# Rows of v in two column halves: stores, gathers, splits and the last products of a graph transformer layer

## The reference, cut to what matters

```
x = x + gnn(layernorm(x)) + mix(layernorm(x))
def fff(x, node_w, node_b, w1, b1, w2, b2):        # tree of depth 4, 16 leaves of width 64
    leaf = route(x, node_w, node_b)
    hidden = relu(x @ w1[leaf] + b1[leaf])
    return hidden @ w2[leaf] + b2[leaf]
q, k, v = fff(h, q_...), fff(h, k_...), fff(h, v_...)      # h = layernorm(x)
attn = softmax(q @ k.T / 32)                               # 384 x 384
x = x + attn @ v                                           # 384 x 1024
```

## Time and profile before

| | us |
|---|---|
| median of 3 runs | 727.94 (725.6 to 729.39) |
| the profiled execution, its own time | 726.86 |
| its span (first to last instruction) | 725.1 |
| PE busy | 702.6 (97%) |
| DVE busy | 476.5 (66%) |
| ACT busy | 402.0 (55%) |
| POOL busy | 229.2 (32%) |
| mean granted TensorE clock | 0.997 of full speed |

### The profile page before, as it was taken

The page is one execution under the profiler, slowest core; times in us unless marked ns, Lnnn a source line. Parts: engine busy times, 40 slices in busy tenths (PEclk is TensorE's granted clock), DMA queues, the critical chain, the costliest instruction groups (busy, mean ns, idle before and its releaser), DMA issues.

```text
span 725.1 us, 11736 instructions
## 1 busy us (share of the span) xinstructions
PE 702.6 (97%) x4490; PEld 669.4 (92%) x4490; DVE 476.5 (66%) x957; ACT 402.0 (55%) x692; POOL 229.2 (32%) x203
## 2 busy tenths in 40 slices
PE   3999999999999999999999999999999998999987
PEld 3989999998999999999999999998899998889886
DVE  6758774874777477766666565656766466787543
ACT  5455556464565565768686775422523457677340
POOL 4634332232332332227022274470004511422120
PEclk9999999999999999999999999999999999999998
DMA  5421635413313223231313152234135749896242
GB/s 212 160 107 59 231 138 211 176 60 120 109 67 117 73 102 117 90 118 58 117 59 117 59 209 73 109 121 138 41 136 193 272 164 378 307 413 220 117 145 88
DMA packets 21766, 105.15 MB, mean 145 GB/s; under 512 B 5696, under 2 KB 6080, under 8 KB 12912
## 3 DMA queue, kind: packets, MB, share of 16 engines
q1 hardware_dynamic: 12880, 80.84, 30.4%
q0 software_dynamic: 8544, 23.41, 8.9%
q10 hardware_dynamic: 288, 0.14, 0.1%
HBM read 92.71 MB, written 18.06 MB: 153 GB/s over the span
## 4 chain that ended last, share of the span: by engine, by line
PE 87%; DVE 6%; ACT 3%; DMA 2%; issue 1%; DVEq 0%; ACTq 0%
PE g_bank L1772 37%; PE g_bank L1797 12%; PE o_bank L1847 4%; PE t_bank L1836 4%; PE s_bank L2150 2%; PE s_bank L1824 2%; PE s_bank L1825 2%; PE g_bank L1726 2%; PE s_bank L2398 2%; PE s_bank L2360 2%; PE s_bank L2358 2%; PE s_bank L2359 2%; PE t_bank L2150 2%; DVE w_lo L1138 1%; PE g_bank L2332 1%; PE t_bank L2251 1%
## 5 line engine op out<-in xcount | busy, mean ns | idle before, releaser
L1772 PE MATMUL g_bank<-act_hi,w_hi 128*128 128x384 f32 x488 | 170.0, 348 | 0.0
L1772 PE MATMUL g_bank<-act_hi,w_lo 128*128 128x384 f32 x488 | 163.7, 335 | 0.0
L1772 PE MATMUL g_bank<-act_lo,w_hi 128*128 128x384 f32 x488 | 163.4, 335 | 0.0
L1138 DVE TENSOR_TENSOR w_lo<-raw,w_hi 128x2048 fp32r<-128x2048 f32 x58 | 137.3, 2367 | 36.0 <-ACT w_hi L675 34.0
L675 ACT ACTIVATE w_hi<-raw 128x2048 fp32r<-128x2048 f32 x67 | 128.1, 1912 | 30.3 <-PE s_bank L2150 12.5
L490 POOL DMA_INDIRECT edge_table<-ew,eidx x51 | 68.2, 1336 | 164.3 <-DMA edge_table<-ew,eidx 158.0
L1772 PEld LDWEIGHTS g_bank<-act_hi,w_hi 128*128 128x128 f32 x488 | 91.8, 188 | 2.7 <-issue 2.6
L1772 PEld LDWEIGHTS g_bank<-act_lo,w_hi 128*128 128x128 f32 x488 | 91.9, 188 | 0.0
L1772 PEld LDWEIGHTS g_bank<-act_hi,w_lo 128*128 128x128 f32 x488 | 91.6, 188 | 0.0
L437 POOL TENSOR_TENSOR w_lo<-raw,w_hi 128x2048 fp32r<-128x2048 f32 x10 | 47.0, 4695 | 103.5 <-ACT w_hi L675 97.2
L1275 DVE TENSOR_TENSOR pT_lo<-t_bank,pT_hi 128x384 fp32r<-128x384 f32 x96 | 50.6, 554 | 33.6 <-ACT pT_hi L768 33.2
(11 more groups left out here) (324 smaller groups left out, 1643.5 us busy)
## 6 DMA issues: line engine op xcount, KB each, us to landing
raw<-wstream_dram SPq DMA_DIRECT2D x68, 1024.0 KB, 4.8
xg<-xs POOLq DMA_DIRECT2D x12, 512.0 KB, 7.9
ys<-y_ring POOLq DMA_DIRECT2D x12, 512.0 KB, 4.6
x_sb<-x_dram SPq DMA_DIRECT2D x3, 512.0 KB, 5.0
y_acc<-x_dram POOLq DMA_DIRECT2D x3, 512.0 KB, 5.7
out_dram<-out_sb SPq DMA_DIRECT2D x6, 256.0 KB, 2.0
edge_table<-ew,eidx POOLq DMA_INDIRECT x51, 2.5
edge_table<-mask POOLq DMA_DIRECT2D x1, 576.0 KB, 3.5
```

Source lines behind the costliest of these rows:

```text
L1138: V.tensor_tensor(flat(w_lo[to][:, :, :]), raws[raw_slot(n.base)], flat(w_hi[to][:, :, :]), ALU.subtract) \
L1772: last = mm(out, w2[a], x2[b], start=k == 0 and a + b == 0, stop=not after and k == KT - 1 and a == 1)
```

## The change

The ring of v rows is the same, but every step behind it works on half a tile's columns:

- Stores: for each of pairs 6 to 11 POOL stores the first half as soon as ACT has taken it (waits for y_act only), then the second half (waits for y_dve), into two DRAM arrays yv[0] and yv[1] of 512 columns. `take_y` of pairs 9 to 11 waits for the store of its own half only.
- Gathers: the first halves of the three tiles (when all first halves are stored and k's transposes are done), then the second halves. Six indirect DMAs of 128 x 512 in place of three of 128 x 1024.
- Splits: ACT and DVE split the three first halves between the softmax of tiles 0 and 1, and the second halves later.
- Products: LAST gives their order: (tile 0, first half), (tile 1, first half), (0, second), (1, second), (2, first), (2, second). The first needs only the first halves of v (vf_ready of 3), the third needs all six. `last_T(2)` moves one product later, and DVE's `take_last(2)` moves behind the first sum.

```diff
+V_PAIRS = 1 * PAIRS
+LAST = ((0, 0), (1, 0), (0, 1), (1, 1), (2, 0), (2, 1))
...
+            def store_v(i, half):
+
+                p = i - V_PAIRS
+                pool.wait_ge((y_act, y_dve)[half], i + 1)
+                pool.dma_start(yv[half][p * P:(p + 1) * P, :], y_at[i][:, half * 512:(half + 1) * 512]) \
+                    .then_inc(v_out[half][p % NT], 16)
+
+            def bring_v(half):
+
+                if half == 0:
+                    pool.wait_ge(kT_full, K_FILLS)
+                for s in v_out[half]:
+                    pool.wait_ge(s, 16 * (PAIRS // NT))
+                for t in range(NT):
+                    nc.gpsimd.indirect_dma_start(y_ring[:, t, half * 512:(half + 1) * 512], None, yv[half],
+                                                 rows_of(2, t), bounds_check=ROWS - 1,
+                                                 oob_is_err=False).then_inc(v_in[half][t], 16)
...
-            for i in range(PAIRS, 2 * PAIRS):
-                store_pair(i)
-            bring_back(1)
+            for i in range(V_PAIRS, V_PAIRS + PAIRS):
+                for half in range(2):
+                    store_v(i, half)
+            for half in range(2):
+                bring_v(half)
...
-            def take_v(t):
-                act.wait_ge(back_in[t], 32)
-                nc.scalar.activation(vf_hi[:, t, :], y_ring[:, t, :], ACT.Copy).then_inc(vf_hi_ready, 1)
+            def take_v(half, t):
+                cols = slice(half * 512, (half + 1) * 512)
+                act.wait_ge(v_in[half][t], 16)
+                nc.scalar.activation(vf_hi[:, t, cols], y_ring[:, t, cols], ACT.Copy).then_inc(vf_hi_ready, 1)
...
             last_exp(0)
+            act.wait_ge(y_full, 2 * (V_PAIRS + PAIRS))
+            for t in range(NT):
+                take_v(0, t)
             last_exp(1)
-            take_v(0)
+            take_v(1, 0)
+            take_v(1, 1)
             take_last(0)
-            take_v(1)
-            take_v(2)
+            take_v(1, 2)
             last_exp(2)
...
             normalise(pf_ring, Index(S_FFN0), 0)
+            for t in range(NT):
+                take_v(0, t)
             last_max(1)
             normalise(pf_ring, Index(S_FFN0 + 1), 1)
-            take_v(0)
+            take_v(1, 0)
+            take_v(1, 1)
             take_last(0)
-            take_v(1)
             last_max(2)
-            take_v(2)
+            take_v(1, 2)
             normalise(pf_ring, Index(S_FFN0 + 2), 2)
             take_last(1)
-            take_last(2)
...
+                if i == 1:
+                    take_last(2)
...
-            for i in range(2 * NT):
-                t, half = divmod(i, 2)
+            for i, (t, half) in enumerate(LAST):
                 c, cols = slice(t * P, (t + 1) * P), slice(half * 512, (half + 1) * 512)
                 if i == 0:
                     pe.wait_ge(h_ready, 2 * PAIRS)
                     pe.wait_ge(vf_ready, NT)
+                if i == 2:
+                    pe.wait_ge(vf_ready, 2 * NT)
...
-                if i == 1:
+                if i == 2:
                     last_T(2)
```

More of the change, by code:

```diff
@@ L228, with program @@
 TTR_START = 3.0e38
-def program(nc, x, wstream, ecols, pp_in, table, w1m, w2m, bo, bout, nodes, leaf_b, xs, xsel, ys, out):
+def program(nc, x, wstream, ecols, pp_in, table, w1m, w2m, bo, bout, nodes, leaf_b, xs, xsel, ys, yv, out):
     with ExitStack() as ctx:
@@ L387, in program @@
         kT_full, kT_hi_ready, kT_ready = sem("kT_full"), sem("kT_hi_ready"), sem("kT_ready")
+        v_out = [[sem(f"v_out{h}{i}") for i in range(NT)] for h in range(2)]
+        v_in = [[sem(f"v_in{h}{t}") for t in range(NT)] for h in range(2)]
         vf_hi_ready, vf_ready = sem("vf_hi_ready"), sem("vf_ready")
@@ L424, in _ @@
                 sp.dma_start(raws[raw_slot(n)], wstream[n]).then_inc(raw_in[raw_slot(n)], 16)
-            for i in range(2 * NT):
-                t, cols = i // 2, slice(i % 2 * 512, i % 2 * 512 + 512)
+            for i, (t, half) in enumerate(LAST):
+                cols = slice(half * 512, half * 512 + 512)
                 sp.wait_ge(out_ready, i + 1)
@@ L1031, in take_y @@
             def take_y(i):
-                if i >= NT:
+                if i >= V_PAIRS + NT:
+                    act.wait_ge(v_out[0][i % NT], 16)
+                elif i >= NT:
                     act.wait_ge(y_out[i % NT], 16 * (i // NT))
@@ L1687, in last_max, with take_v @@
                  .then_inc(e_in, 1)
-            def take_v(t):
-                dve.wait_ge(vf_hi_ready, t + 1)
-                V.tensor_tensor(vf_lo[:, t, :], y_ring[:, t, :], vf_hi[:, t, :], ALU.subtract).then_inc(vf_ready, 1)
+            def take_v(half, t):
+                cols = slice(half * 512, (half + 1) * 512)
+                dve.wait_ge(vf_hi_ready, NT * half + t + 1)
+                V.tensor_tensor(vf_lo[:, t, cols], y_ring[:, t, cols], vf_hi[:, t, cols], ALU.subtract) \
+                 .then_inc(vf_ready, 1)
             def take_last(t):
@@ L2530 @@
     args["table"] = nc.dram_tensor("edge_table", (N * N, 1), F32).ap()
-    for name, shape in (("xs", (ROWS, D)), ("xsel", (ROWS, LEAVES)), ("ys", (ROWS, D))):
-        args[name] = [nc.dram_tensor(f"{name}{f}", shape, F32).ap() for f in range(2)]
+    for name, count, shape in (("xs", 2, (ROWS, D)), ("xsel", 2, (ROWS, LEAVES)), ("ys", 1, (ROWS, D)),
+                               ("yv", 2, (ROWS, 512))):
+        args[name] = [nc.dram_tensor(f"{name}{f}", shape, F32).ap() for f in range(count)]
     args["out"] = nc.dram_tensor("out_dram", (N, D), F32, kind="ExternalOutput").ap()
```

6 lines of the change are left out of this document (3 added, 3 removed).

## The result

The changed kernel took 723.33 us (median of 6 runs, 722.35 to 723.71), beside 726.78 (725.38 to 729.39) for the kernel before on the same chip: ratio 0.9938, 95% interval 0.9921 to 0.9955, which is 3.3 to 5.7 us faster. The profiled execution took 722.35 (before: 726.86), its span is 720.6.

A forecast was written before the change was run, and what follows sets the result against it. The splitting of v was taken to bound the end, leaving PE idle 3.25 us and then slow. Terms 2.77 + 1.46 - 0.5 gave 3.7, with overlaps 3.85: 727.94 to 724.1 us, 8-in-10 range 722.9 to 726.3.

The forecast's parts named there:

- The gathers' timing: Half gathers on POOL start at 693.4, 1.33 apart; the third first half lands 3.4 to 3.5 us after its start.
- The chain on ACT and DVE: DVE's maximum of tile 1 ends the wait at 700.85, first product at 704.85 (gain 2.77), second product waits 0.5.
- Why v is late: POOL's timeline: Before the first product, v is late because pair 11's store delays the gathers; the third lands at 704.5.
- The clock term, 1.46: First product, slow at clock 0.50 after PE's 3.25 us idle, falls from 3.52 to 2.06 us at full clock.
- The chances: For the whole kernel: faster 0.52, within 0.5% 0.44, slower 0.04; the forecast of 724.1 itself 0.63.
- Rival 1: Last gathers held by DVE's vf_lo, or slower by up to 1 us: gain 2.7 to 2.9, 725.1; chance 0.18.
- Rival 2: PE's clock still falls at the first product after two pauses of about 0.5: gain 2.8, 725.4; chance 0.07.
- Rivals 3 and 4: Half gathers take a whole one's 2.0 us: 727.9, chance 0.08; six gathers cost POOL more than three: 731.2, chance 0.04.

The follow-up runs named there:

- second profile: The changed kernel run and profiled again, unedited: median 723.35 us, ratio 0.9944 to the kernel before.
- Transport alone: Kernel before with only the change's half-column stores and six gathers; splits, products and order as before: median 727.58 us, ratio 0.9996.
- splits alone: Kernel before with v split by halves, tile 0's ahead of its transposed softmax, tile 2's maximum behind all splits; stores and gathers whole: 723.81 us, ratio 0.9952.
- the run with two inputs: Changed kernel plus one useless 128x2048 DVE subtraction, both inputs in SBUF, behind DVE's last copy of v: median 724.2 us, ratio 0.9957.
- the changed kernel with one DVE input: Changed kernel plus one useless 128x2048 DVE sum with one SBUF input, behind DVE's last copy of v: median 723.41 us, ratio 0.9941.

## Why the prediction was right and wrong

*The gathers' timing:* right. Spacing 1.30 to 1.33 for 1.33; the third first half landed 3.22 and, in the second profile, 3.79 after its start for 3.4 to 3.5; the first gather 1.03 behind the last store's start for 0.9.

*The chain on ACT and DVE:* right. DVE's second maximum came 7.44 and 7.79 us after the first gather's start in the two profiles (forecast 7.45), the first product 11.35 and 11.70 after it (11.45). The gain there was 3.11 and 2.77 (2.77), the pause before the second product 0.24 and 0.25 (0.5).

*"Why v is late: POOL's timeline":* wrong, although the size fitted; this is the step of the mechanism that failed. I had the chain of waits and read only its last three links, then argued from the stores and gathers of the earlier trace rows because they were visibly late. The chain went through tile 0's transposes at 702.67, ACT's pTf_hi and the whole-tile splits behind it. Transport alone gives 0.1 us; splits alone give 3.9 of the 4.3, clock included. So early gathers alone could not have ended the pause that I laid to them. My sum came near, in part by luck, because it followed the changed kernel's whole path, in which early gathers and re-ordered splits come together.

*The clock term, 1.46:* wrongly sized, and this is the step that failed in the number. It was read from one execution. Over the runs the loss is none in a quarter and about 2.5 us in the rest (727.98 - 725.52). At full clock the change gains 725.52 - 723.35 = 2.2 (forecast 2.4 without the clock term); the other 2.1 of the median is the clock. So the medians differ by 4.3 where I had 3.85, and I forecast 724.1 for a kernel that runs at 723.3.

*The chances:* with the forecast 0.2 under the bound of 0.5%, I gave 0.44 to no change and took before's spread of 3.8 us for scatter of the measurement. It was two groups, of which the change removes one. The three times that I had (725.6, 727.94, 729.39) were too few to show it.

*Rival 1 (gathers held by vf_lo):* the mechanism is real, as the run with two inputs shows, but was not met. Each first half of vf_lo begins 0.2 to 0.3 after a gather's start: DVE starts at 697.12, 698.33 and 699.62, POOL at 696.80, 698.11 and 699.41. A gather with a subtraction inside it still took 1.00. The Trainium skill, page "SBUF — State Buffer", section "SBUF: two separate sides", says that whichever starts first keeps the shared port for its whole instruction. By that rule, the traces agree for the gathers: the one that came second waited, the one that came first did not. The same sentence of the page says that the other fully blocks, and for DVE as the second the traces do not agree: the three subtractions that begin inside a gather last 0.68 to 0.69, as the one at 704.57, with no gather near, does (0.68). Whether the gather reads SBUF in that stretch no run shows. What a wait costs a gather is the rest of the subtraction: 0.76 in the run with two inputs, up to 2.1 for k's gathers.

*Rival 2 (clock):* did not happen. Its counter-evidence was weak, however: behind the pause at 610 to 612, clock 1.00 in the earlier trace rows, 5 of the 15 profiles of the experiments show the lower level, as this row of the changed kernel with one DVE input:

```profile
613.00:614.00 1.00, 1.00 (x7) 0.50 1.03 426
```

Its run took 723.27 us, no more than others: DMA moves 390 to 470 GB/s there, its share of time is about 1, and PE has just been idle. That PE has slack there is my reading, not shown by a run of its own.

*Rivals 3 and 4:* excluded by the spacing of 1.30 and the landings of 3.2 to 3.9 of the gathers by halves.

## What to carry to other kernels

Follow the chain of waits back past its last links before saying which transfer is late: a transfer that does not stand in it can start 3 us earlier for nothing, while moving a split past a wait for PE pays at once. The early transfer may pay once the order behind it is changed (here 0.9 us). Where a pause of TensorE stands near 3 us, take the clock's price from many runs, not from one profile: group the runs' times by their granted clock; the kernel's own spread tells what removing the pause is worth. Work that does not depend on the engine one waits for (here the second half of tile 0's v) belongs in front of that wait.

## What the runs showed of the hardware

- The same pause of TensorE (3.23 us) was followed by full clock in one execution and by some 5.7 us at 0.50 in another. Ahead of the products, pauses of 1.5 to 1.7 us left 33 of the 36 runs of four kernels in one quick group each.
- An indirect DMA's start that falls into a DVE subtraction with two SBUF inputs ends 0.86 to 0.97 us behind the subtraction's end (19 cases in 17 profiles); one that falls into a DVE sum of equal length with one input takes its usual 1.07. A DVE subtraction that begins inside a gather is not held (0.68).
- A gather of 128 rows of 2 KB lands 3.2 to 3.9 us after its start (4.2 where a subtraction held it up), one of 4 KB rows 4.5 to 5.9; both hold POOL for 1.0 to 1.1 where no subtraction holds them up.
